# Cross-attention and routed experts on one core: projection columns reordered, query parts stacked from SBUF, the opening re-ordered

## The chip, the cores and the metric

The kernel runs on 1 core of one Trainium2 chip. The metric is the device time of one execution in microseconds (us), the median over runs. Engines: TensorE (PE), with its weight loads shown apart as PEld; VectorE (DVE); ScalarE (ACT); GpSimd (POOL); SyncE (SP), which here only issues transfers.

## What is computed

Sixteen batches of 112 rows and 256 columns attend to a context of 375 rows each; then every row goes through two of eight experts. Cut to what matters here:

```python
q = split_heads(layernorm(x) @ Wq.T + bq)      # 16 heads of 16 columns
k = split_heads(ctx @ Wk.T + bk)
v = split_heads(ctx @ Wv.T + bv)
scores = einsum('bhqd,bhkd->bhqk', q, k) / 4   # masked rows of ctx: -1e9
x = x + softmax(scores) @ v @ Wo.T + bo
x = x + top2_of_8_experts(layernorm(x))        # silu(x @ w1) @ w2, weighted
```

## The kernel before, in words

**Precision in parts.** Each operand of a product is cut into a high part and a low part (the rest), and a product is three matmuls: high x high, low x high, high x low. ACT writes high parts, DVE or POOL writes low parts.

**Stacked scores.** For a batch, the keys (`kh`, `kl`, 128 partitions x 2 x 376) are copied by DMA, SBUF to SBUF, into `ks[ring]`: 96 partitions hold (half of the heads, dimension of the head, part), and 8 head pairs lie along the row. The queries go into `qs[ring]` in the same way, so that one matmul of 98 rows gives a head's scores with all parts. Partitions 96 to 99 hold the mask and the row maxima. There are three rings. The keys take 6 transfers a batch (3 parts, each in 2 halves). The queries of the first batch take 6 transfers straight from SBUF; those of all others go through DRAM: `write_queries(g)` writes 6 pieces of a group of 4 batches to `q_scratch`, and `stack_queries` brings a batch back with 2 transfers. SP issues all of these in an order written by hand.

**Turns.** After the opening, PE runs a loop `turn(b)` over the 16 batches. In it lie the 16 `head_scores` of batch b+1 (DVE takes the maximum of each, `maxima`), the 4 `quad_scores` of batch b (ACT takes the exponentials), the outputs of b, the values of b+1 and the keys of b+3. The experts' stage follows after the last batch.

**The opening** (about the first 54 us) normalises x in 4 groups, transposes it, projects queries of the 4 groups, the keys of the first three batches and the values of the first, and takes the row maxima of the first batch. Each engine's order is a hand-written list of calls: `x_stats` (DVE), `x_std` (ACT, square root), `roots` (DVE), `normalise_x` (ACT), `x_transpose` (PE), `x_high` (ACT), `x_low` (DVE), `project_queries` (PE), `q_high` (ACT: `qf` and `qh`, both halves of the columns), `query_low` (POOL). `qf` is one buffer. `qh` and `ql` have two buffers each, so `q_high(g)` of groups 2 and 3 waits until the group before last has been written to DRAM. PE waits for all of `qh` before turn 0.

Of the kernel before, what the change touches and what calls it, by code (L numbers as in the profile page):

```python
# [5 lines left out]
F32 = mybir.dt.float32  # L6
# [21 lines left out]
GB = 4  # L28
# [77 lines left out]
def xattn_moe_kernel(nc, x_rows, x_tiles, ctx_t, mask, wq_t, wk_t, wv_t, wo_t, bq, bk, bv, bo,  # L106
                     router_w, w1, w2, out):
    ctx = ExitStack()
    with ctx:
# [19 lines left out]
        tl = sb("attn_t_lo", [P, KD, T], F32R)  # L129
        hidden_end = cursor["at"]  # L130
# [48 lines left out]
        def expert_buffers(p):  # L179
# [40 lines left out]
        qf = sb("q_f32", [P, KD, SG])  # L220
        qh = [sb(f"q_hi{p}", [P, KD, SG], F32R) for p in range(2)]
        ql = [sb("q_lo0", [P, KD, SG], F32R)]
        last_query_at = cursor["at"]
        ql.append(sb("q_lo1", [P, KD, SG], F32R))
# [6 lines left out]
        assert cursor["at"] <= xr_at + 4 * (B * D + KD * SG), "the last key stack lies where x and q were"  # L231
# [6 lines left out]
        assert cursor["at"] <= queries_end, "the third context lies where the queries' parts were"  # L238
# [88 lines left out]
        q_scratch = nc.dram_tensor("q_scratch", [KD, DK, PARTS, HALF, T], F32).ap()  # L327
# [9 lines left out]
        q_written = [sem(f"q_written{p}") for p in range(2)]  # L337
        bias_in, vo_bias_in, xr_first_in, xr_rest_in, rw_in = (sem(n) for n in (
            "bias_in", "vo_bias_in", "xr_first_in", "xr_rest_in", "rw_in"))
# [69 lines left out]
        def queries_stacked(b):  # L409

            return 48 * (b.lap + 1) + (64 if b.ring == 0 else 0)

        def queries_written(g):

            return 96 * (g // 2 + 1)

        def first_stack(queue, c, src):
            for a in range(2):
                row = PARTS * DK * a
                queue.dma_start(qs[0][row + c:row + PARTS * DK:PARTS, :, S * a:S * (a + 1)].bitcast(F32),  # L420
                                src[:, a, 0:S].bitcast(F32)).then_inc(q_stacked[0], 16)

        @block.sync
        def _(sp):
# [13 lines left out]

            def stack_queries(b):
# [5 lines left out]
                if not early(b, 1):  # L445
                    sp.wait_ge(q_written[b.n // GB % 2], queries_written(b.n // GB))
                    for a in range(2):
                        row = PARTS * DK * a
# [3 lines left out]
                if b.n == RINGS - 1:  # L452
                    sp.wait_ge(xt_done, NG)
                    sp.wait_ge(ql_ready, NG)
                sp.dma_start(ks[b.ring][R_MASK:ROWS, :, :].bitcast(F32),
                             mask_scratch[b.n:b.n + 1, :, :].rearrange("a p n -> p a n")
                             .to_broadcast([4, HALF, CP])).then_inc(q_stacked[b.ring], 16)

            def stack_keys(b):

                for c, src in enumerate((kh, kh, kl)):
                    if c != 1:
                        sp.wait_ge((kh_ready, kl_ready)[c // 2], b.n + 1)
                    for a in range(2):
                        row = PARTS * DK * a
                        sp.dma_start(ks[b.ring][row + c:row + PARTS * DK:PARTS, :, :].bitcast(F32),  # L466
                                     src[:, a, :].bitcast(F32)).then_inc(k_stacked[b.ring], 16)
# [9 lines left out]
            def turn(b):  # L477
                if has(b.after(2)):
                    stack_queries(b.after(2))
                    stack_keys(b.after(2))  # L480
                if b.n < 2:
                    write_queries(b.n + 2)
# [7 lines left out]
            def load_rows(group, done):  # L490
                sp.dma_start(xr[:, group, :], x_rows[group].rearrange("b s d -> s b d")).then_inc(done, 16)
# [4 lines left out]
            def write_queries(g):  # L496
                sp.wait_ge(qh_ready, KD * (g + 1))
                sp.wait_ge(ql_ready, g + 1)
                for c, src in enumerate((qh, ql, qh)):
                    for t in range(KD):  # L500
                        sp.dma_start(q_scratch[t, :, c, :, SG * g:SG * g + SG],  # L501
                                     src[g % 2][:, t, :].bitcast(F32)).then_inc(q_written[g % 2], 16)

            second = first.after(1)
            load_rows(slice(0, GB), xr_first_in)
# [5 lines left out]
            sp.dma_start(bv_c[:, :], bv).then_inc(bias_in, 16)  # L511
            sp.wait_ge(keep_ready, 1)
            sp.dma_start(keep_scratch, keep_all[:, :]).then_inc(mask_written, 16)
            load_rows(slice(GB, 2 * GB), xr_rest_in)
            sp.wait_ge(mask_written, 16)
            load_keep(0, slice(0, 2))
            load_ctx(second)
            load_weight(2, wv_t)
            sp.wait_ge(xr_rest_in, 16)
            load_rows(slice(2 * GB, B), xr_rest_in)  # L520
            sp.wait_ge(mask_rows_ready, 1)
            sp.dma_start(mask_scratch, m_rows[:, :, :].bitcast(F32)).then_inc(mask_written, 16)
# [1528 lines left out]
```

## Time and profile before

| | us |
|---|---|
| median of 3 runs | 471.98 (471.88 to 472.85) |
| profiled execution, its own time | 471.65 |
| its span in the profile | 469.9 |
| PE busy | 413.5 (88%) |
| DVE busy | 339.6 (72%) |
| ACT busy | 277.0 (59%) |
| POOL busy | 223.0 (47%) |

Times below are microseconds from the start of the span. A matmul's duration includes its overlap with the next one; the granted clock is given as a share of 2.4 GHz, so 0.50 is 1.2 GHz.

### The profile page before, as it was taken

How to read it: one execution, taken by the hardware profiler on the slowest of the kernel's cores; microseconds unless marked ns; L12 is line 12 of the kernel's file. 1: busy time of each engine (PE TensorE's matmuls, PEld its weight loads, DVE VectorE, ACT ScalarE, POOL GpSimd, SP SyncE). 2: the span in 40 equal slices, each digit the busy share in tenths (PEclk: the TensorE clock that was granted, in tenths of full speed). 3: DMA queues.
4: the chain of work that ended last, by engine and by line, in shares of the span. 5: the costliest groups of instructions: out<-in, count | busy, mean ns of one | idle time of the engine just before them, and what ended most of it. 6: DMA issues, size and time to landing. Idle time of an engine off the chain costs nothing.

```text
span 469.9 us, 10766 instructions
## 1 busy us (share of the span) xinstructions
PE 413.5 (88%) x4187; PEld 384.6 (82%) x4187; DVE 339.6 (72%) x699; ACT 277.0 (59%) x373; POOL 223.0 (47%) x252
## 2 busy tenths in 40 slices
PE   2767599999999999999999999589989999999820
PEld 2655489999999999999988898589989999999810
DVE  6746367878888787888877958965676777767545
ACT  3547356666655766565564462547767777788600
POOL 6554324332234444222322473844887787786420
PEclk9979889999999999999999996569999999999985
DMA  7999398867688777668670139912222222332169
GB/s 187 226 240 232 124 242 175 227 142 167 131 183 188 159 149 172 142 121 165 134 131 9 47 117 371 339 48 67 80 81 85 83 91 91 78 88 73 46 209 305
DMA packets 60307, 69.83 MB, mean 149 GB/s; under 512 B 19265, under 2 KB 55378, under 8 KB 60258
## 3 DMA queue, kind: packets, MB, share of 16 engines
q1 hardware_dynamic: 54018, 56.02, 49.1%
q0 software_dynamic: 4032, 11.02, 7.9%
q10 hardware_dynamic: 2208, 2.12, 1.3%
q8 instruction: 33, 0.54, 0.5%
q14 instruction: 16, 0.13, 0.1%
HBM read 35.29 MB, written 14.78 MB: 107 GB/s over the span
## 4 chain that ended last, share of the span: by engine, by line
PE 73%; DMA 8%; DVE 7%; issue 3%; ACT 3%; POOL 2%; SPq 2%; POOLq 0%; DVEq 0%; ACTq 0%
PE ps L1556 36%; PE ps L1617 11%; PE ps L1632 9%; PE ps L1646 9%; PE ps L1919 2%; PE ps L1659 1%; DMA q_scratch<-q_hi 1%; DMA k_stack<-k_lo 1%; DMA y_rows<-y_out,slot_of_row 1%; DMA w_raw<-wv_t 1%; DMA y_back<-y_rows 1%; SPq L501 1%; DMA rows<-xn_rows,token_of_row 1%; POOL rows L780 1%; SPq L466 1%
## 5 line engine op out<-in xcount | busy, mean ns | idle before, releaser
L1119 DVE TENSOR_REDUCE neg_max<-ps 112x1 f32<-112x376 f32 x256 | 133.5, 545 | 42.5 <-PE ps L1617 37.6
L852 ACT ACTIVATE probs<-ps 125x1344 f32<-125x1344 f32 x64 | 82.8, 1293 | 42.9 <-PE ps L1632 37.7
L1617 PE MATMUL ps<-k_stack,q_stack 98*112 98x376 f32 x256 | 87.5, 376 | 7.0 <-ACT q_hi L891 4.6
L619 POOL TENSOR_TENSOR k_lo<-k_f,k_hi 128x752 fp32r<-128x752 f32 x16 | 28.9, 1804 | 115.5 <-ACT k_hi L826 115.5
L780 POOL DMA_INDIRECT rows<-xn_rows,token_of_row x42 | 55.0, 1310 | 19.0 <-issue 12.2
L1617 PEld LDWEIGHTS ps<-k_stack,q_stack 98*112 98x112 f32 x256 | 45.3, 179 | 19.0 <-DVE neg_max L1119 9.9
L788 POOL DMA_INDIRECT y_rows<-y_out,slot_of_row x42 | 47.3, 1126 | 27.0 <-ACT y_out L1046 15.7
L1632 PE MATMUL ps<-q_stack,k_stack 100*125 100x224 f32 x384 | 53.0, 274 | 0.1
L1632 PEld LDWEIGHTS ps<-q_stack,k_stack 100*125 100x125 f32 x384 | 51.0, 190 | 0.9 <-ACT probs L852 0.5
L1556 PE MATMUL ps<-w_hi,h_hi 128*128 128x256 f32 x168 | 48.7, 290 | 1.6 <-issue 1.6
L1556 PE MATMUL ps<-flat_t_hi,w_hi 128*128 128x256 f32 x168 | 47.6, 283 | 2.0 <-DVE flat_t_lo L1443 2.0
L1556 PE MATMUL ps<-flat_t_hi,w_lo 128*128 128x256 f32 x168 | 47.2, 281 | 0.0
L1556 PE MATMUL ps<-flat_t_lo,w_hi 128*128 128x256 f32 x168 | 47.2, 281 | 0.0
L1556 PE MATMUL ps<-w_hi,h_lo 128*128 128x256 f32 x168 | 47.0, 280 | 0.0
L1556 PE MATMUL ps<-w_lo,h_hi 128*128 128x256 f32 x168 | 47.0, 280 | 0.0
L1646 PE MATMUL ps<-probs,v_wide 125*32 125x112 f32 x1536 | 47.0, 262 | 0.0
L1646 PEld LDWEIGHTS ps<-probs,v_wide 125*32 125x32 f32 x1536 | 35.1, 109 | 8.0 <-issue 5.6
L1027 ACT ACTIVATE h_f<-ps 128x1024 f32<-128x1024 f32 x21 | 21.6, 1027 | 25.8 <-PE ps L1556 25.8
L1556 PEld LDWEIGHTS ps<-flat_t_hi,w_hi 128*128 128x128 f32 x168 | 31.9, 190 | 2.4 <-DVE flat_t_lo L1443 2.4
L610 POOL TENSOR_TENSOR ctx_lo<-ctx_raw,ctx_hi 128x752 fp32r<-128x752 f32 x15 | 27.2, 1812 | 13.5 <-ACT ctx_hi L819 13.5
L1556 PEld LDWEIGHTS ps<-w_hi,h_hi 128*128 128x128 f32 x168 | 31.8, 189 | 2.0 <-issue 1.8
L1465 DVE TENSOR_TENSOR h_lo<-h_f,h_hi 128x1024 fp32r<-128x1024 f32 x21 | 25.7, 1225 | 10.2 <-ACT h_hi L1032 10.2
(209 smaller groups left out, 1023.6 us busy)
## 6 DMA issues: line engine op xcount, KB each, us to landing
k_stack<-k_hi SPq DMA_DIRECT2D x64, 188.0 KB, 4.6
w_all<-w SPq DMA_DIRECT2D x2, 4096.0 KB, 18.1
k_stack<-k_lo SPq DMA_DIRECT2D x32, 188.0 KB, 5.6
ctx_raw<-ctx_t SPq DMA_DIRECT2D x32, 187.5 KB, 5.1
q_stack<-q_scratch SPq DMA_DIRECT2D x30, 168.0 KB
q_scratch<-q_hi SPq DMA_DIRECT2D x16, 224.0 KB, 4.6
y_back<-y_rows SPq DMA_DIRECT2D x14, 256.0 KB, 4.8
q_scratch<-q_lo SPq DMA_DIRECT2D x8, 224.0 KB, 4.4
```

What stands on the lines that cost most here:

```text
L610: pool.tensor_tensor(cl[home][:, :, :], c_raw[b.par][:, :, :], ch[home][:, :, :].bitcast(F32), ALU.subtract).then_inc(cl_ready, 1)
L619: pool.tensor_tensor(kl[:, :, :], kf[:, :, :], kh[:, :, :].bitcast(F32), ALU.subtract)\
L780: pool.indirect_dma_start(rows[t.ring][:, a, :], None, xn_rows, row_of(token_i, t, a))\
L788: pool.indirect_dma_start(y_rows, row_of(slot_i, t, a), yo[t.par][:, a, :], None)\
L852: act.activation(pf[j % 2][:, :, :], ps[0:CT, BK_ST:BK_ST + KT, 0:4 * S], ACT.Exp).then_inc(pf_ready, 1)
L1027: act.activation(hf[t.par][:, :, :], silu_source(t), ACT.Silu).then_inc(hf_ready, 1)
L1119: dve.tensor_reduce(neg_max[:, s:s + 1], ps[0:S, BK_MAX + s % 2, 0:CP], AX.X, ALU.max, negate=True).then_inc(max_read, 1)
L1465: dve.tensor_tensor(hl[t.par][:, :, :], hf[t.par][:, :, :], hh[t.par][:, :, :].bitcast(F32), ALU.subtract).then_inc(hl_ready, 1)
L1556: last = pe.matmul(o, lhs, rhs, start=first and n == 0, stop=final and n == len(terms) - 1)
L1617: pe.matmul(ps[0:S, BK_MAX + a, 0:CP], qs[b.ring][0:R_MAX, q, S * a:S * (a + 1)], ks[b.ring][0:R_MAX, q, :], start=True, stop=True).then_i ...
L1632: last = pe.matmul(ps[0:CT, BK_ST + k3, 2 * S * q:2 * S * (q + 1)], ks[b.ring][0:ROWS, 2 * j + q, k3 * CT:(k3 + 1) * CT], qs[b.ring][0:ROW ...
L1646: last = pe.matmul(ps[VC * i:VC * (i + 1), BK_OUT, S * j:S * (j + 1)], vx[b.par][:, k3, 2 * j + i // 2 + HALF * (i % 2), :], pf[j % 2][:, ...
```

## The change

- The columns of the query and key weights and biases are put in another order (`by_dim`), so that a partition of the projected keys holds two head pairs that are neighbours in the stack. A key part is then one transfer over 128 partitions, 3 a batch and not 6.
- `q_scratch`, `write_queries` and the DRAM detour go. `qh` and `ql` now lie in the buffers `th` and `tl` (where the attention's output comes later), one place for each group, and a batch's queries are stacked from there by 6 transfers.
- The opening is re-ordered on all five engines. `q_high` and `first_query_low` are called by halves; keys of the first batch are cut before the value weights; the output weights and the router's weights are loaded, cut and their low parts taken before the first maxima; x comes in 4 loads; the table for exponentials is loaded behind the last square root; on PE the query products go ahead of the heads of the first batch; the wait for all of `qh` moves to the first `quad_scores`.
- PE runs 16 matmuls of the identity with itself, whose result is not read, ahead of the first transposes.

In the diff below, SP's part comes first, then ACT's list of the opening from the first keys on as it stands after the change, DVE's, PE's and the host's. The calls of `write_queries` for groups 1 to 3 go as the one shown does.

```diff
         def queries_stacked(b):
-            return 48 * (b.lap + 1) + (64 if b.ring == 0 else 0)
+            return 112 * (b.lap + 1)
...
+            def stack_part(b, c, src):
+                for a in range(2):
+                    row = PARTS * DK * a
+                    half = P // 2 * a
+                    sp.dma_start(qs[b.ring][row + c:row + PARTS * DK:PARTS, :, S * a:S * (a + 1)].bitcast(F32),
+                                 src[half:half + P // 2, :, S * b.n:S * (b.n + 1)].bitcast(F32))\
+                        .then_inc(q_stacked[b.ring], 16)
             def stack_queries(b):
...
-                        sp.dma_start(qs[b.ring][row:row + PARTS * DK, :, S * a:S * (a + 1)].bitcast(F32),
-                                     q_scratch[a, :, :, :, S * b.n:S * (b.n + 1)].rearrange("d c q n -> (d c) q n"))\
-                            .then_inc(q_stacked[b.ring], 16)
+                g = b.n // GB
+                sp.wait_ge(qh_ready, KD * (g + 1))
+                stack_part(b, 0, th)
+                stack_part(b, 2, th)
+                sp.wait_ge(ql_ready, g + 1)
+                stack_part(b, 1, tl)
...
             def stack_keys(b):
-                    for a in range(2):
-                        row = PARTS * DK * a
-                        sp.dma_start(ks[b.ring][row + c:row + PARTS * DK:PARTS, :, :].bitcast(F32),
-                                     src[:, a, :].bitcast(F32)).then_inc(k_stacked[b.ring], 16)
+                    sp.dma_start(ks[b.ring][c:KD * PARTS * DK:PARTS, :, :].bitcast(F32), src[:, :, :].bitcast(F32))\
+                        .then_inc(k_stacked[b.ring], 16)
...
-            write_queries(0)
...
             load_rows(2)
             sp.wait_ge(mask_rows_ready, 1)
             sp.dma_start(mask_scratch, m_rows[:, :, :].bitcast(F32)).then_inc(mask_written, 16)
+            load_weight(3, wo_t)
+            sp.dma_start(rw_raw[:, :, :], router_w.rearrange("k p n -> p k n")).then_inc(rw_in, 16)
+            sp.wait_ge(mask_written, 32)
+            stack_mask(first)
+            stack_keys(first)
+            stack_queries(first)
+            load_rows(3)
             load_ctx(first.after(2))
+            sp.wait_ge(filled, 4)
+            stack_queries(second)
+            stack_mask(second)
+            stack_keys(second)
...
+            key_high(first)
             attn_weight(2)
+            q_high(0, 0)
             x_std(1)
+            q_high(0, 1)
             normalise_x(1)
+            x_high(1)
             x_std(2)
+            normalise_x(2)
             key_high(second)
             attn_weight(3)
             act.wait_ge(rw_in, 16)
             act.copy(rw[:, :, 0:E], rw_raw[:, :, :]).then_inc(rw_ready, 1)
+            x_high(2)
+            values(first, True)
+            values(first, False)
+            x_std(3)
+            act.activation(root_c[:, :], eps_c[:, :], ACT.Exp)
+            q_high(1, 0)
+            normalise_x(3)
+            q_high(1, 1)
+            ctx_high(first.after(2))
+            q_high(2, 0)
+            x_high(3)
+            q_high(2, 1)
+            key_high(first.after(2))
+            q_high(3, 0)
+            q_high(3, 1)
...
+            attn_weight_low(2)
             x_stats(2)
+            roots(2)
             x_low(1)
+            attn_weight_low(3)
+            dve.wait_ge(rw_ready, 1)
+            dve.tensor_tensor(rw[:, :, E:2 * E], rw_raw[:, :, :], rw[:, :, 0:E].bitcast(F32), ALU.subtract)\
+                .then_inc(rw_ready, 1)
             maxima(first, range(0, 2))
...
+                    for n in range(16):
+                        pe.matmul(ps[:, BK_SPIN, 0:P], ident[:, :], ident[:, :], start=True, stop=True)
...
             for n, part in enumerate(all_parts):
+                project_queries(1, (part,))
                 head_scores(first, range(2 * n, 2 * n + 2))
-                project_queries(1, (part,))
             for n, part in enumerate(all_parts):
-                head_scores(first, range(8 + 2 * n, 8 + 2 * n + 2))
-                if n == 3:
-                    max_transpose(first)
                 project_queries(2, (part,))
                 if n == 2:
                     x_transpose(3)
+                head_scores(first, range(8 + 2 * n, 8 + 2 * n + 2))
+            max_transpose(first)
             for t in range(KD):
                 project_keys(first.after(2), t)
             project_queries(3)
-            pe.wait_ge(qh_ready, KD * NG)
...
     def by_dim(w):
-        return np.ascontiguousarray(w.reshape(w.shape[0], KD, HALF, DK).swapaxes(2, 3)).reshape(w.shape)
+        heads = w.reshape(w.shape[0], 2, HALF // KD, KD, DK)
+        return np.ascontiguousarray(heads.transpose(0, 3, 1, 4, 2)).reshape(w.shape)
```

## Rows read from the trace of the kernel before

**Rows 1.** The page: busy time, share and instructions; granted clock in 40 slices.

```profile
PE 413.5 (88%) x4187; PEld 384.6 (82%) x4187; DVE 339.6 (72%) x699; ACT 277.0 (59%) x373; POOL 223.0 (47%) x252
...
PEclk9979889999999999999999996569999999999985
```

**Rows 2.** Busy time by stretch: stretch, length, each engine, granted clock, DMA share, GB/s.

```profile
16.20:24.80 8.60, 6.14 (x40) 4.94 (x38) 7.41 (x25) 5.23 (x10) 6.42 (x6) 1.00 0.89 189
...
28.60:34.10 5.50, 5.46 (x19) 4.59 (x20) 3.10 (x6) 3.02 (x6) 4.42 (x3) 0.51 1.00 320
49.90:54.40 4.50, 0.00 (x0) 0.00 (x0) 0.00 (x0) 2.18 (x5) 0.00 (x0) 1.00 0.38 101
...
54.50:70.20 15.70, 14.16 (x97) 12.52 (x97) 11.34 (x20) 7.16 (x9) 6.78 (x10) 0.78 0.73 191
...
84.00:97.70 13.70, 13.70 (x177) 12.56 (x181) 11.01 (x25) 8.62 (x11) 3.56 (x2) 1.00 0.83 186
```

**Rows 3.** The chain of waits in order of time: start, duration, what.

```profile
21.45 5.64 DMA k_stack<-k_lo
...
46.49 5.66 DMA q_scratch<-q_hi
...
70.26 1.29 PE ps L1646 x48
...
83.99 1.29 PE ps L1646 x48
...
86.70 0.71 PE ps L1646 x24
```

**Rows 4.** Timeline: start, duration, engine, line, operation, tiles, idle time before.

```profile
12.98 0.52 PE L1556 MATMUL ps<-ctx_lo,attn_w_hi 128*128 128x376 f32 x1
...
13.76 0.34 PE L1556 MATMUL ps<-ctx_lo,attn_w_hi 128*128 128x376 f32 x1
...
15.26 1.49 DVE L1093 TENSOR_TENSOR attn_w_lo<-w_raw,attn_w_hi 128x512 fp32r<-128x512 f32 x1 [1.92 <-ACT attn_w_hi L803]
...
54.48 0.66 PE L1617 MATMUL ps<-k_stack,q_stack 98*112 98x376 f32 x1 [4.61 <-ACT q_hi L891]
54.50 2.10 POOL L643 TENSOR_TENSOR q_lo<-q_f,q_hi 128x896 fp32r<-128x896 f32 x1 [7.15 <-ACT q_hi L891]
...
54.97 2.18 DVE L1093 TENSOR_TENSOR attn_w_lo<-w_raw,attn_w_hi 128x512 fp32r<-128x512 f32 x1 [6.84 <-ACT attn_w_hi L803]
```

**Rows 5.** Timeline of SP's queue: start, time to issue, transfers.

```profile
10.34 0.55 SPq L522 DMA_DIRECT2D mask_scratch<-mask_rows  x1
...
18.15 2.61 SPq L466 DMA_DIRECT2D k_stack<-k_hi  x4
```

**Rows 6.** Transfers by line, first 62 us: count, KB each, median us to landing.

```profile
mask_scratch<-mask_rows SPq DMA_DIRECT2D x1, 94.0 KB, 8.1
```

**Rows 7.** ACT's groups of instructions, first 62 us: busy us, mean ns, idle before.

```profile
L875 ACT ACTIVATE x_rows_sb<-x_rows_sb,less_mean,rstd 112x256 f32<-112x256 f32 x12 | 6.2, 592 | 1.0 <-DVE less_mean L1167 1.0
L891 ACT ACTIVATE q_hi<-ps,bq_c 128x448 fp32r<-128x448 f32 x8 | 4.9, 628 | 0.0
...
L826 ACT CAST k_hi<-k_f 128x752 fp32r<-128x752 f32 x3 | 2.5, 819 | 7.3 <-DVE k_f L1103 4.3 <-DMA k_stack<-k_lo 3.1
...
L852 ACT ACT_TABLE_LOAD x1 | 1.3, 1283 | 0.0
```

**Rows 8.** The same view, DVE's groups.

```profile
L1119 DVE TENSOR_REDUCE neg_max<-ps 112x1 f32<-112x376 f32 x23 | 11.6, 541 | 8.7 <-PE ps L1617 8.4
L1156 DVE BATCH_NORM_STATS2 stats<-x_rows_sb 112x6 f32<-112x256 f32 x16 | 5.6, 409 | 1.7 <-DMA x_rows_sb<-x_rows 1.7
...
L1178 DVE TENSOR_TENSOR x_t_lo<-ps,x_t_hi 128x896 fp32r<-128x896 f32 x4 | 4.4, 1088 | 4.1 <-ACT x_t_hi L870 4.1
```

**Rows 9.** The same view, POOL's groups.

```profile
L643 POOL TENSOR_TENSOR q_lo<-q_f,q_hi 128x896 fp32r<-128x896 f32 x3 | 6.3, 2103 | 11.8 <-ACT q_hi L891 11.8
L619 POOL TENSOR_TENSOR k_lo<-k_f,k_hi 128x752 fp32r<-128x752 f32 x3 | 5.4, 1789 | 5.3 <-ACT k_hi L826 5.3
```

More of the change, by code:

```diff
@@ L129, in xattn_moe_kernel @@
         tl = sb("attn_t_lo", [P, KD, T], F32R)
+        qh = [th[:, :, SG * g:SG * (g + 1)] for g in range(NG)]
+        ql = [tl[:, :, SG * g:SG * (g + 1)] for g in range(NG)]
         hidden_end = cursor["at"]
@@ L219, in xattn_moe_kernel @@
         xr = sb("x_rows_sb", [S, B, D])
[L220 to L224, printed above, removed]
+        cursor["at"] = last_query_at = xr_at + 4 * (B * D + 4 * KD * SG)
+        cursor["at"] += 4 * KD * SG
         queries_end, cursor["at"] = cursor["at"], xr_at
@@ L230, in xattn_moe_kernel @@
         last_ring_end = cursor["at"]
-        assert cursor["at"] <= xr_at + 4 * (B * D + KD * SG), "the last key stack lies where x and q were"
+        assert cursor["at"] <= xr_at + 4 * (B * D + KD * SG), "the last key stack lies where x was"
         cursor["at"] = third_ctx_at = xr_at + first_queries
@@ L237, in xattn_moe_kernel @@
         third_ctx_end = cursor["at"]
-        assert cursor["at"] <= queries_end, "the third context lies where the queries' parts were"
+        qf = sb("q_f32", [P, KD, SG])
+        assert cursor["at"] <= queries_end, "the queries come before the flat rows"
         cursor["at"] = queries_end
@@ L488, in _, with load_rows @@
             first = Batch(0, 0)
-            def load_rows(group, done):
-                sp.dma_start(xr[:, group, :], x_rows[group].rearrange("b s d -> s b d")).then_inc(done, 16)
+            def load_rows(g):
+                group = slice(GB * g, GB * (g + 1))
+                sp.dma_start(xr[:, group, :], x_rows[group].rearrange("b s d -> s b d")).then_inc(xr_in[g], 16)
             def load_weight(n, w):
                 sp.dma_start(wraw[n], w.rearrange("k p n -> p k n")).then_inc(aw_in[n], 16)
[L496 to L502, printed above, removed]
             second = first.after(1)
-            load_rows(slice(0, GB), xr_first_in)
+            load_rows(0)
             sp.wait_ge(zeros_set, 1)
@@ L814, in ctx_high @@
                 else:
-                    if b.n == 6:
-                        for g in range(NG - 2, NG):
-                            act.wait_ge(q_written[g % 2], queries_written(g))
                     act.wait_ge(vproj_done, 2 * (b.n - 2))
@@ L1202, in _ @@
             keys(first, 0)
-            attn_weight_low(2)
             keys(first, 1)
@@ L1627, in quad_scores @@
                     pe.wait_ge(mx_stacked[b.ring], 32 * (b.lap + 1))
-                if not (early(b, 1) and j < 1):
+                if early(b, 1) and j < 1:
+                    pe.wait_ge(qh_ready, KD * NG)
+                else:
                     pe.wait_ge(pf_ready, QUADS * b.n + j)
```

126 lines of the change are left out of this document (34 added, 92 removed).

## The prediction

> **What bounds the kernel now.** I began with the page: PE is busy for 88% of the span, no other engine for more than 72% [rows 1]. The row of granted clock beneath it shows where PE is not at its best: three places, one near the start, one near the middle, one at the end [rows 1]. The change touches the first. In the stretches, a turn of the main loop takes 13.7 us, PE is busy for all of it and its clock is full [rows 2]. So in the turns nothing that another engine or a transfer does is worth time unless it comes too late. The opening is another matter: head 0 of turn 0 starts only at 54.48, after 4.61 us in which PE waited [rows 4]. In the stretch 49.90 to 54.40 PE does nothing at all [rows 2]. The chain of waits names what it waited for: a DMA into `q_scratch`, 5.66 us long, from 46.49 [rows 3], which kept `q_high(3)` from its buffer. Ahead of that the chain holds the last key part of the first batch, 5.64 us from 21.45 [rows 3]; ACT's `key_high(second)` stood behind it with the whole list that follows. After both, PE starts at half clock, 0.51 in 28.60 to 34.10 [rows 2]. Turn 0 shows what else is wrong: DVE's low part of the output weights is in the way of its maxima (2.18 us at 54.97 [rows 4]), and from head 0 to the outputs at 70.26 it takes 15.8 us at a mean clock of 0.78 [rows 2, 3, 4].
>
> The end of the change's reach is therefore that row at 70.26, where turn 1 begins in full swing. Every later turn is bound by PE, so what is gained there should reach the end unshortened.
>
> **The first 24 us.** The 16 unread products fill PE from the identity's making to about the first normalised rows. Before, matmuls of 376 columns took 0.52 us at 12.98 and 0.34 at 13.76 [rows 4]: that is where the clock rose. Some ten key products at half clock lie ahead of that, each about 0.15 us longer, so 1.5 us of PE time goes. It is hidden for the most part: the first keys also wait for the mask's broadcast, which lands no earlier. What moves the keys is the order: `k_f`'s second half now waits neither for the value weights nor for their low part (1.49 us from 15.26 [rows 4]), so I put `kh` of the first batch at 14.7 where its stacking began at 18.15 [rows 5]. It does not get all of this. SP now waits for `mask_scratch` first. That was issued at 10.34 and landed 8.1 us later, at 18.4 [rows 5, 6], behind 896 KB of x. Now 448 KB of it lie ahead, and at some 250 GB/s (the stretches show 189 to 320 [rows 2]) the other half is 1.8 us: 16.6. With the mask's own copy the keys begin at 17.2. Three transfers of 0.65 us each to issue [rows 5], not six. Their bytes are the same. Six took from 18.15 to 27.09, 8.9 us [rows 3, 5]; at the 189 GB/s of that stretch [rows 2] the 1.13 MB are 6.1. So they land between 23.3 and 26.1, and I take 24.2, near the lower end, since half of the issues and the DRAM writes behind them are gone. The second group's and third group's rows are normalised by about 24.0 on ACT, so nothing is lost by waiting.
>
> The Trainium skill bears on this (DMA: Bandwidth & Descriptors, Rules for kernel authors): two transfers to disjoint partition halves run one after the other over the same engines, so one transfer over 128 partitions is to be used. By that the keys' merger gives only issue time, and the queries' new halves cost issue time; no run here shows it yet, and neither the landing above nor the sum rests on it.
>
> **From 24.2 to turn 0.** One chain, each step by its row. ACT `kh` of the second batch 0.82, POOL `kl` 1.79 [rows 7, 9]; DVE's `attn_weight_low(3)` runs beside it. At 54.97 that operation took 2.18 us beside POOL's 2.10 from 54.50, so it ended 0.55 after POOL did [rows 4]: I let it end 0.55 after `kl`. With the router's parts 0.2: DVE is free for maxima at 27.6. The Trainium skill has the rule (SBUF — State Buffer, Who interferes with whom): a VectorE instruction with two SBUF inputs and a GpSimd one that reads SBUF block each other. The trace agrees, by the 2.18; without the rule this step would end about 1 us sooner. It speaks against putting the weights ahead of the maxima.
>
> DVE then: four maxima at 0.54, `x_low(2)` 1.09, `x_stats(3)` 1.4 and its aggregates 0.3 [rows 8], 5.0 in all: 32.6. ACT: square root 0.3, the exponentials' table 1.28 (it used to stand in turn 0 at no cost and is now on the path) and its dummy 0.2, `q_high(1,0)` 1.2, normalising four batches 2.07 (6.2 for 12), `q_high(1,1)` 1.2 [rows 7]: 6.3, so 38.9. PE has been held by `project_queries(2)`, which needs the banks that `q_high(1)` empties, and the heads 12 to 15 stand behind it. PE: one part 0.6, eight transposes 0.9, a pair of heads 0.35, four maxima 2.2, the transpose of the maxima 0.3: 43.2. Keys of the third batch, 12 products of 376 columns, 2.05, and queries of group 3, 12 of 448, 2.4, at full clock: 47.7. Beside it POOL does `query_low(1)` 2.1 and the third context's low part 1.8 [rows 9] from 38.9, ready at 42.8, just in time for the keys. The chain `q_high(2)`, `query_low(2)`, `q_high(3)` ends at about 48.9; the wait for it now stands at the first `quad_scores`, some 3.6 us into turn 0 (51.3), so it is covered by 2.4 us. The row maxima of the first batch are sent at 43.9 and needed there too. Head 0 of turn 0 starts at 47.7 for 54.48: **6.8 us**. The bounds of the key landing (23.3, 26.1) make it 7.7 or less to 4.9.
>
> **Turn 0.** A whole turn is 13.73 from 70.26 to 83.99 [rows 3]. Turn 0 has no outputs of a batch before, three times 0.71 [rows 3], nor its transposes, some 0.6. That is 11.0 of PE work. DVE has 16 maxima of 0.54 and two key halves, 9.9, and the first heads go at its pace. I take 12.2; the ends are 11.0 and 13.7. Before it was 15.8: **3.6 us** (2.1 to 4.8). The cover here is a warm PE, which has had no long pause since 42.
>
> **In the turns** PE has no slack but the rest has. SP issues 4 more query transfers (2.6 us by 0.65 each) and 3 fewer for keys (1.95): 0.65 us later, in a turn in which DMA is busy for 0.83 of 13.7 and so 2.3 us free [rows 2, 5]. Costed at nothing. The work that leaves (24 writes to DRAM) was on the path only at 46.49 [rows 3], counted above.
>
> Sum: 6.8 + 3.6 = 10.4. The profiled execution took 471.65, its span 469.9. 461.25; the median of the runs shown lies 0.33 above that execution: 461.6, which I round to 461.5.
>
> **Rivals.**
> *PE goes cold in the first batch's heads.* Between 25 and 37 it has short work between waits for DVE: some 5 us of 12. In 16.20 to 24.80 6.14 of 8.60 kept the clock at 1.00; 4.50 of nothing lost it [rows 2]; the case between is not in the trace. It would cost doubled parts, transposes and heads from 33 to 43, about 2.2, then the keys and queries of 43.2 on at half clock (the stretch at 0.51 lasted 5.5 us before the clock came back [rows 2], half of that lost: 2.7): 4.9, so 466.4. The Trainium skill (TensorE: Matmul & The Clock Gate, A second HAM failure mode) says that small idle times between groups of matmuls can make the clock go up and down; by that this rival is the forecast. I give it 0.2.
> *A wait takes the place of the one removed.* POOL's and ACT's query chain passes everything through one `qf`, and key landing at its upper end shifts it all by 1.9; if x of group 3, now loaded behind the first queries, comes after 31 as well, each us counts in full. 3 to 7 us of gain remain: 465 to 469. 0.13.
> *The gain is hidden.* That needs the third batch's keys to come late for turn 1: `kl` of it stands behind `query_low(3)`. I have it stacked at 58 for 59.9. For no gain at all it must be 12 us late. 0.03.
> *Slower: queries from SBUF overload the DMA in the turns.* 768 pieces a batch, now read from SBUF where 2 transfers read DRAM. It decides from 2.3 us more DMA work a turn on, and outweighs the opening above 3.1 (0.8 times 13 turns). At 3.5 it gives 461.5 + 13 x 1.2 = 477. For it: the DMA share of 0.83. Against it: the pieces are as many and as large as before, and the keys' pieces may become fewer. 0.06.
> *More than forecast:* turn 0 at 11.0 and keys at 23.3: 458. 0.08.
>
> **How the numbers follow.** Forecast 0.50, with its own range of 459 to 464. From the other cases: 457.5 below, 468 above leaves out some 0.15. Two runs of this kernel differ by up to 0.2%, 1 us, and less counts as no change. Faster by more than 0.2%: 0.89; within: 0.04; slower: 0.07.
>
> **What would show it.** Right: no row into `q_scratch`; PE busy from 2 us and key products at 0.34 from the first; head 0 of turn 0 near 47.7 at clock 1.00; the first maxima near 27.6; an idle PE around 36 to 38.9 waiting for `q_hi`; the x48 outputs near 59.9; turns of 13.7. Wrong: granted clock 0.5 between 27 and 45; a turn longer than 13.8 with PE waiting for a stack; first maxima after 29.

## The result, and the profile after

The kernel after takes 467.17 us (median of 4 runs, 466.05 to 468.23), the kernel before, measured beside it, 471.93 (4 runs, 471.34 to 472.85). The ratio is 0.9897, with a 95% interval of 0.9868 to 0.9926. So 4.8 us were gained where 10.4 were forecast. The profiled execution took 468.23, the longest of the four, with a span of 466.3 for the 469.9 of before. The readings below are made against that span.

The first lines to read are the same three of the page as in [rows 1]:

```profile
PE 418.5 (90%) x4219; PEld 388.8 (83%) x4219; DVE 340.3 (73%) x699; ACT 278.1 (60%) x374; POOL 223.4 (48%) x252
...
PEclk9868999999999999999999996569999999999965
```

They say little: PE is busy for 5 us more in a span 3.6 us shorter, and the first digits of the granted clock are lower, not higher. What tells more is the start of a turn in full swing, the x48 row of [rows 3]. In the chain of waits of the kernel after it comes at these times (start, duration, what):

```profile
61.68 1.29 PE ps L1622 x48
...
146.24 1.29 PE ps L1622 x48
...
231.58 1.29 PE ps L1622 x48
```

Turn 1 starts at 61.68 for the 70.26 of [rows 3]: 8.6 us gained in the opening. The row at 231.58 is twelve turns on: 169.9 us, 14.16 a turn on average, single ones 13.7 to 15.5. Before, a turn took 13.73 [rows 3], twelve of them 164.8. So 5.1 us of the 8.6 are lost again in the turns; 3.5 remain, and the spans differ by 3.6.

The chain shows the loss where a turn's first head is due, behind the x48 row:

```profile
161.32 1.70 issue
163.02 0.40 PE ps L1591
```

"issue" is time for which the view finds no releaser. The table of waits over 62 to 228 has it as the largest of PE's weight loads (us in total, times, longest):

```profile
PEld ps L1591 <- issue: 7.2, 12, 1.9
```

In the kernel before, and in the kernels below whose turns take 13.73, the same row reads 2.1 to 2.2 us. The excess over it is 5.1, the whole loss.

What PE waited for is read from SP's queue, here the transfers of the turn that starts at 146.24 (start, time to issue, transfers):

```profile
147.64 1.51 SPq L531 DMA_DIRECT2D x<-x_tiles  x1
149.24 2.57 SPq L437 DMA_DIRECT2D q_stack<-attn_t_hi  x4
151.86 1.25 SPq L437 DMA_DIRECT2D q_stack<-attn_t_lo  x2
153.15 0.49 SPq L429 DMA_DIRECT2D k_stack<-mask_scratch  x1
153.69 1.22 SPq L459 DMA_DIRECT2D k_stack<-k_hi  x2
154.96 0.61 SPq L459 DMA_DIRECT2D k_stack<-k_lo  x1
```

and from the landing time of the last of them (count, KB, us from issue to landing):

```profile
k_stack<-k_lo SPq DMA_DIRECT2D x1, 376.0 KB, 8.0
```

The keys' first transfer is issued at 153.69, 7.45 after the turn's start; the last, at 154.96, lands 8.0 later, at 162.96. The first head that reads them was due at 161.32 and ran at 163.02. In the kernel before, the same block stands like this in SP's queue, in the turn that starts at 152.62:

```profile
153.99 0.58 SPq L549 DMA_DIRECT2D x<-x_tiles  x1
154.67 1.92 SPq L449 DMA_DIRECT2D q_stack<-q_scratch  x2
156.63 0.51 SPq L455 DMA_DIRECT2D k_stack<-mask_scratch  x1
157.18 2.52 SPq L466 DMA_DIRECT2D k_stack<-k_hi  x4
159.75 1.25 SPq L466 DMA_DIRECT2D k_stack<-k_lo  x2
```

There the keys start 4.56 into the turn, and the last of its two `k_lo` transfers, 5.7 us on its way, lands at about 166.1, when the head is due at 167.6 (15.0 after the turn's start). Of the 2.9 us between 7.45 and 4.56, 1.9 are the queries' issues (3.82 for 1.92) and 0.9 the load of `x` ahead of them, which took 1.51 to issue here and 0.58 there. Over all twelve turns the keys start 5.9 to 7.7 us into the turn, 6.9 on average, where they started 3.2 to 4.8 in, 4.0 on average.

The reader should also see the cost of an issue: 0.64 us for 56 KB (2.57 for four), 0.61 for 376 KB. The transfer's size does not show in it, though a single issue can take more than twice as long, as that of `x` did. Meanwhile the DMA engines are not full. The stretch of the six query transfers and that of the keys behind it, one turn later (each engine's busy time, granted clock, DMA share, GB/s):

```profile
162.00:166.70 4.70, 3.68 (x45) 3.28 (x46) 2.33 (x5) 2.59 (x5) 2.79 (x2) 1.00 0.46 130
166.70:175.70 9.00, 9.00 (x95) 8.46 (x97) 7.92 (x18) 4.65 (x6) 2.02 (x2) 1.00 0.86 184
```

Over the twelve turns the DMA share fell, while the turns became longer. The kernel before and the kernel after:

```profile
70.26:235.09 164.83, 164.83 (x2081) 151.27 (x2084) 132.12 (x288) 102.82 (x130) 53.82 (x91) 1.00 0.75 161
61.68:231.58 169.90, 165.00 (x2080) 151.23 (x2084) 132.07 (x288) 103.71 (x130) 53.70 (x91) 1.00 0.66 148
```

SP's queue is not full either. The table of SP's own waits in the kernel after (us in total, times, longest) has one row over 62 to 228:

```profile
SPq L466 <- DVE max_rows L1103: 45.0, 12, 5.1
```

On average 3.75 us of each turn SP waits for the row maxima of the next batch, and the queries and keys of the batch behind it stand in the list after that wait. Whether they could be issued ahead of it was not tried.

The opening after the change, in pieces of the chain of waits:

```profile
9.96 5.86 DMA mask_scratch<-mask_rows
16.20 0.70 SPq L459
...
17.58 7.99 DMA k_stack<-k_lo
...
27.02 1.90 DVE attn_w_lo L1066
29.01 0.92 DVE neg_max L1092 x2
...
33.78 1.28 ACT L892
...
39.51 1.42 PE ps L1530 x3
...
44.30 4.56 PE ps L1530 x24
```

Each of these has its place in the forecast: the mask's landing, the keys, the low part of the output weights, the first maxima, the exponentials' table, a part of the query products of group 2, the keys of the third batch. Head 0 of turn 0 starts at 48.70 (54.48 in [rows 4]); 47.7 was forecast. The stretches show that PE did go cold on the way:

```profile
20.00:24.00 4.00, 4.00 (x24) 4.00 (x23) 2.60 (x11) 3.17 (x6) 1.94 (x2) 0.57 1.05 192
24.00:28.00 4.00, 1.91 (x10) 1.41 (x9) 0.98 (x1) 2.47 (x6) 1.41 (x1) 0.89 1.13 277
28.00:32.00 4.00, 3.85 (x11) 2.46 (x10) 4.00 (x8) 0.65 (x2) 3.49 (x3) 0.50 0.77 155
```

### The profile page after: what moved, and what is told of

The parts are those of the page before. It is cut to its first block, busy times and chain, and to the rows that moved or that the text cites. A ratio compares the mean times of both kernels' runs of the same rounds, so it can differ in the third digit from the quotient of the medians.

```text
span 466.3 us, 10813 instructions
## 1 busy us (share of the span) xinstructions
PE 418.5 (90%) x4219; PEld 388.8 (83%) x4219; DVE 340.3 (73%) x699; ACT 278.1 (60%) x374; POOL 223.4 (48%) x252
## 4 chain that ended last, share of the span: by engine, by line
PE 76%; DVE 8%; DMA 7%; issue 3%; ACT 3%; SPq 1%; POOL 1%; ACTq 0%; POOLq 0%; DVEq 0%
PE ps L1530 39%; PE ps L1591 12%; PE ps L1608 9%; PE ps L1622 9%; PE ps L1895 2%; DMA k_stack<-k_lo 2%; PE ps L1635 2%; DMA mask_scratch<-mask_rows 1%; DMA y_rows<-y_out,slot_of_row 1%; DMA y_back<-y_rows 1%; DVE neg_max L1092 1%; PE ps L1691 1%; DMA keep_scratch<-keep_all 1%; PE ps L1701 1%; PE ps L1647 1%
## 5 line engine op out<-in xcount | busy, mean ns | idle before, releaser
L1530 PEld LDWEIGHTS ps<-w_lo,h_hi 128*128 128x128 f32 x168 | 31.9, 190 | 0.0
```

What stands on the lines that cost most here:

```text
L1530: last = pe.matmul(o, lhs, rhs, start=first and n == 0, stop=final and n == len(terms) - 1)
```

## The experiments

All times are medians with their range; the ratio is to the kernel before on the same chip, with its 95% interval. The runs were spread over several chips, on which the median of the kernel before was 471.5 to 472.5, so kernels are compared by their ratios, and a difference of 1 us between two medians can be the chip's. "Head 0" is the start of head 0 of turn 0, "first row" the x48 row with which turn 1 begins in full swing.

### Where the turns lose: the order behind SP's queue

Three ways were open: the keys are issued too late (order), the merged key transfers land later than six small ones (size), or the DMA engines have too much to do (amount).

**Keys between the queries' parts.** From the first turn on SP issues the four high query transfers, then the keys, then the two low ones and the mask.

```diff
-                    stack_queries(b.after(2))
-                    stack_mask(b.after(2))
-                    stack_keys(b.after(2))
+                        stack_queries(b.after(2), low=False)
+                        stack_keys(b.after(2))
+                        stack_part(b.after(2), 1, tl)
+                        stack_mask(b.after(2))
```

> Edit: in the turns SP issues the four high query transfers, then the three key parts, then the two low query transfers and the mask; nothing else differs from the changed kernel. Theory A (the six query transfers stand ahead of the keys in SP's order and make the key stack land after head 0 of the next turn is due): the key parts are issued about 1.8 us earlier in a turn, head 0 no longer waits, all turns take 13.7 to 13.8 us, and the 5.1 us that twelve turns had lost come back: about 462 us. Theory B (one transfer of 376 KB for a key part is slow in itself, since its landing takes 7.1 us where 188 KB took 5.7): the block of keys still ends late and the turns stay uneven; under 1.5 us is gained, 466 to 467.

464.10 us (463.84 to 465.83, 4 runs); ratio 0.9845 (0.9809 to 0.9881). The first row comes at 61.22, the one twelve turns later at 227.94: 166.7, where the kernel after has 169.9. The same transfers in another order give back 3.2 of 5.1 us. The keys start 5.05 us into a turn on average for 6.9, and `k_lo` has a median of 6.1 us to landing for 7.1: the order acts through both. What is left has a name now:

```profile
PEld ps L1597 <- DMA k_stack<-mask_scratch: 3.2, 7, 0.9
```

The mask had been put last, and is late next. It was not tried alone; "Together" below moves it, and the rest of the loss is gone.

**Four query transfers fewer.** From the fourth batch on the high query parts are not stacked (left out of the computation); everything else stays in its order, so the keys come four issues earlier.

```diff
-                stack_part(b, 0, th)
-                stack_part(b, 2, th)
+                if early(b, RINGS):
+                    stack_part(b, 0, th)
+                    stack_part(b, 2, th)
```

> Leaves out part of the work: from the fourth batch on only the low part of the queries is stacked, the two high parts are not, so four of six query transfers of a turn are gone. Theory A: keys are issued 2.6 us earlier, every turn takes 13.7, about 462 us. Theory B: the keys are the same large transfers, so the turns stay uneven and it gives 465 or more.

463.49 us (462.73 to 463.86, 4 runs); ratio 0.9825 (0.9794 to 0.9855).

```profile
61.87 1.29 PE ps L1623 x48
...
226.60 1.29 PE ps L1623 x48
```

164.73 for twelve turns, 13.73 each: all of the loss is gone. Yet a `k_lo` transfer of 376 KB takes as long as in the kernel after: a median of 7.2 us for its 7.1.

So the size of the merged transfers is not what makes a turn long. As 224 KB a turn are gone as well as four issues, this kernel alone does not part order from amount.

**The column order and the merged key transfer alone**, in the kernel before; queries go through DRAM as there.

```diff
-                    for a in range(2):
-                        row = PARTS * DK * a
-                        sp.dma_start(ks[b.ring][row + c:row + PARTS * DK:PARTS, :, :].bitcast(F32),
-                                     src[:, a, :].bitcast(F32)).then_inc(k_stacked[b.ring], 16)
+                    sp.dma_start(ks[b.ring][c:KD * PARTS * DK:PARTS, :, :].bitcast(F32), src[:, :, :].bitcast(F32))\
+                        .then_inc(k_stacked[b.ring], 16)
```

> Edit to the kernel before: only the order of the projection's columns and the key part as one transfer; queries still go through DRAM, the opening is as it was. Theory A: the keys' block takes the same 8.9 us from its first issue to landing with three transfers as with six, nothing in the turns was waiting, so within 0.5 us of before: 471.5 to 472.4. Theory B: keys land later, some turns wait: 474 or more. My prediction's step for the opening (fewer issues make the first keys land earlier) would give 1 us less than before, 471.

470.44 us (468.93 to 471.71, 10 runs); ratio 0.9954 (0.9933 to 0.9976). In its profile head 0 comes at 52.55 and the first row at 68.30, 1.96 before that of [rows 3]; twelve turns take 165.26. In the opening the keys' first transfer is issued at 17.73 and the last lands at 25.69:

```profile
19.61 6.08 DMA k_stack<-k_lo
```

8.0 us for three transfers; six took 8.9 [rows 3, 5]. In the turns its `k_lo` has a median of 8.0 us to landing, the longest of all kernels here, and its turns are not slow: its keys start early. The merger lets the first block land 0.9 sooner, where three issues of 0.6 are saved, and gives about 0.5% of the time.

**Two transfers more.** The kernel after with two extra transfers of 56 KB to DRAM ahead of the keys in each turn.

```diff
                 stack_part(b, 1, tl)
+                if not early(b, RINGS):
+                    for a in range(2):
+                        sp.dma_start(extra[b.n, a], tl[P // 2 * a:P // 2 * (a + 1), :, S * b.n:S * (b.n + 1)].bitcast(F32))\
+                            .then_inc(q_stacked[b.ring], 16)
```

> Edit to the changed kernel: in the turns two more transfers of 56 KB (the low query parts, into a place in DRAM that nobody reads) stand ahead of the keys in SP's order, 1.3 us more to issue. Theory A (what stands ahead of the keys delays the end of the key stack, and head 0 of the next turn waits for it): every turn is now longer than 13.73, by 1 to 1.5 us, the alternating pattern becomes a steady one; twelve turns take 178 to 183 us, the time is 475 to 481. Theory B (the loss comes from the key transfers' own size or from other traffic): the twelve turns stay near 170 and the time near 467 to 469.

476.54 us (475.98 to 478.23, 4 runs); ratio 1.011 (1.007 to 1.0151). Twelve turns take 177.3 (63.21 to 240.47), 14.8 each.

```profile
PEld ps L1596 <- issue: 13.4, 14, 2.4
```

The same wait as in the kernel after, now 13.4 us for 7.2. Its `k_lo` still lands in 7.2 us, and the DMA share over the twelve turns is 0.66, as in the kernel after. Two transfers of 56 KB, 1.3 us of issue, cost 0.6 us a turn. With 2 query transfers ahead of the keys a turn takes 13.73, with 4 13.9, with 6 14.16, with 6 and the two extra ones 14.8 (the 13.9 is the mask's, as "Together" below shows: it has 4 ahead as well and turns of 13.73). The keys' first issue lies 4.0 to 4.1, 5.05, 6.9 and 8.2 us into the turn, on average.

### The opening: what is on the path

**No unread products.** The kernel after without the 16 products of the identity.

```diff
-                    for n in range(16):
-                        pe.matmul(ps[:, BK_SPIN, 0:P], ident[:, :], ident[:, :], start=True, stop=True)
```

> Edit: the changed kernel without the 16 unread products. I expect the first key products at half clock again (0.31 us apart and not 0.17), and the first keys as late as the mask's broadcast lets them be (13.4), so the time within 1 us of the changed kernel, 466.5 to 468. If the clock was on the path, it is 1.5 to 2 us slower than the changed kernel: 468.5 to 469.5.

468.11 us (466.81 to 471.30, 10 runs); ratio 0.9936 (0.9912 to 0.9960). Its interval overlaps that of the kernel after (0.9868 to 0.9926); the span is the same, 466.3, and head 0 comes at 48.57 for 48.70. The products are worth nothing that can be measured here. Its turns are those of the kernel after, and twelve of them took 168.8 in its profile (61.53 to 230.33) for 169.9: the loss differs by 1 us from one execution to the next.

**Output weights ahead of the second batch's keys on ACT**, in the kernel with the keys between.

```diff
-            key_high(second)
             attn_weight(3)
             act.wait_ge(rw_in, 16)
             act.copy(rw[:, :, 0:E], rw_raw[:, :, :]).then_inc(rw_ready, 1)
+            key_high(second)
```

> Base: e1_keys_between. ACT cuts the output weights and the router's before it waits for the key stack (key_high of the second batch), not behind it. Then DVE's low part of the output weights (1.90 us at 27.02, beside POOL's k_lo) runs at about 24.8 while DVE idles, in 0.7 us. If that step was on the path as my prediction has it, the first maxima start 1.1 us earlier (at 27.8 and not 28.9, then bound by the last query transfer that landed at 27.3) and head 0 of turn 0 comes 1 us earlier: 463. If the clock or the ACT chain behind takes it back, 464.

463.80 us (462.45 to 465.62, 4 runs); ratio 0.9837 (0.9794 to 0.9881), in which it can't be told from the kernel it is built on. In the trace it did its work: the first maxima come at 28.07 for 28.81, head 0 at 47.75 for 48.24.

**The exponentials' table back in turn 0.**

```diff
-            act.activation(root_c[:, :], eps_c[:, :], ACT.Exp)
```

> Base: e1_keys_between. The dummy exponential that loads the table behind the last square root is left out, so the table is loaded at the first real exponentials, as before the change. My prediction put its 1.48 us on the path: then head 0 of turn 0 and the time come up to 1.5 us earlier, 462.6, since ACT waits for PE at the first exponentials anyway. If the load now delays the first exponentials, as the author of a preload would hold, nothing or a loss up to 1.3 us: 464 to 465.4.

462.45 us (462.27 to 462.65, 4 runs); ratio 0.9804 (0.9772 to 0.9837). Head 0 comes at 47.73, 0.5 earlier. The median falls by 1.65, but the intervals of the two ratios overlap (0.9809 to 0.9881 for the kernel it is built on). Only a third of the 1.5 us between the two spans shows in the opening; the rest lies in turns that wait less for the mask (2.4 us in that row for 3.2) and behind the turns. In the trace ACT did come earlier: `q_high(1,1)` ends at 38.00 for 39.19. But PE, at half clock, reaches the query part that waits for it only at 38.77, for 39.70, and stays at half clock almost to the end of that part.

**Together:** keys between, output weights first, table late, and in each turn the mask ahead of the queries and the load of `x` (for the experts) behind the context's.

```diff
+                if mask:
+                    stack_mask(b)
                 sp.wait_ge(qh_ready, KD * (g + 1))
```

> Base: e1_keys_between with both edits of e6 and e7, and in the turns the mask's transfer ahead of the queries and the load of x for the residual behind the context's, since head 0 still waits up to 0.9 us in some turns for the mask, which is now the last in the order. Expected: twelve turns in 164.8 us (e1: about 166.7), 2 us less, and 1 to 2.5 us from the opening: 460 to 461. If the opening's two edits have the same place on the path, 461.5.

459.83 us (459.29 to 460.17, 4 runs); ratio 0.9750 (0.9717 to 0.9783). Twelve turns take 164.8 again (58.52 to 223.29), with all six query transfers and all bytes, at a DMA share of 0.63: the whole loss of the turns is one of order. Its keys start 4.9 us into a turn on average.

Head 0 comes at 45.43, 2.8 us before that of the kernel with the keys between, where the two edits of the opening gave 0.5 each alone. 1.0 of it is there at the first maxima (27.78 for 28.81). From these to head 0 it takes 17.65 us, for 19.43 in the kernel with the keys between, 19.68 with the output weights first and 18.60 with the table late. The granted clock is the difference that the rows show, here in 36 to 40 of the kernel with the table late and of this one:

```profile
36.00:40.00 4.00, 4.00 (x15) 3.57 (x14) 2.01 (x4) 2.71 (x5) 1.86 (x1) 0.54 1.03 312
36.00:40.00 4.00, 3.51 (x19) 2.56 (x19) 2.24 (x5) 2.42 (x5) 3.18 (x2) 1.00 0.98 298
```

In the first PE is busy for all 4 us and stands in the chain of waits; in the second it waits for ACT.

**The mask's rows ahead of two loads.** The write of `mask_scratch` goes ahead of the value weights and of the third group of x (704 KB).

```diff
+            sp.wait_ge(mask_rows_ready, 1)
+            sp.dma_start(mask_scratch, m_rows[:, :, :].bitcast(F32)).then_inc(mask_written, 16)
             load_weight(2, wv_t)
             load_rows(2)
-            sp.wait_ge(mask_rows_ready, 1)
-            sp.dma_start(mask_scratch, m_rows[:, :, :].bitcast(F32)).then_inc(mask_written, 16)
```

> Base: e8_together. In the opening SP writes the mask to DRAM ahead of the value weights and of the third group of x, not behind them. In e8 the write went out at 10.28 and landed at 16.0, and the keys' first transfer stood behind it (16.38). If the landing of the first stacks is what the opening waits for (my prediction's step), the first key transfer goes at about 15.3 (kh is ready then), everything to turn 0 moves by 0.8 to 1 us: 459. If DVE's or ACT's list is the bound, no change: 459.8. The value weights come 0.5 us later, which could take some of it back.

457.17 us (456.40 to 457.71, 4 runs); ratio 0.9680 (0.9647 to 0.9713): the fastest kernel of the study, 15 us below before and 10 below after; its interval lies clear of that of "Together" (0.9717 to 0.9783). SP's queue in its opening:

```profile
12.54 0.32 SPq L429 DMA_DIRECT2D k_stack<-mask_scratch  x1
...
17.25 0.55 SPq L462 DMA_DIRECT2D k_stack<-k_lo  x1
```

SP no longer waits for the mask but for the keys themselves, and `k_lo` lands in 5.7 us (7.7 in the kernel it is built on). The first maxima come at 25.41 for 27.78, head 0 at 43.70 for 45.43. The chain of waits has no key transfer left between 10 and 30, and the output weights' low part is short:

```profile
24.67 0.69 DVE attn_w_lo L1072
...
25.45 0.97 DVE neg_max L1098 x2
```

**PE kept busy.** In the kernel "together", unread products of 64 columns between the heads of the first batch: 16 ahead of the first pair, 3 ahead of or behind later ones, into a free bank (the profile counts two matmuls for each). The last ones, behind the heads, are not in the diff shown.

```diff
             for n, part in enumerate(all_parts):
                 project_queries(1, (part,))
+                if n == 1:
+                    pe.wait_ge(vx_ready, 2)
+                unread(3 if n else 16, 6 if n else BK_SPIN)
                 head_scores(first, range(2 * n, 2 * n + 2))
```

> Base: e8_together. 16 unread products of 64 columns while PE waits for the first stacked queries (25.2 to 27.1), and 3 after each of the next pairs' query products, so that PE is not idle between the first batch's heads. My rival said that the cold clock there costs 4.9 us. In e8 the clock is 0.50 in 28 to 32 and 0.84 in 32 to 36, and PE has some 15 products of 448 columns at 0.37 apart and not 0.20 there: 2.5 us of PE time, most of it beside DVE's maxima. If DVE and ACT set the pace, the clock comes to 1.00 and the time stays within 0.5 us of e8 (459.3 to 460.3); if the clock is on the path, 457.5 to 458.5.

460.97 us (460.44 to 461.04, 4 runs); ratio 0.9764 (0.9733 to 0.9794), in which it can't be told from the kernel it is built on (0.9750); nothing is gained. The clock is full:

```profile
28.00:32.00 4.00, 4.00 (x31) 3.88 (x29) 2.96 (x6) 0.27 (x1) 3.74 (x3) 1.00 0.61 159
32.00:36.00 4.00, 3.45 (x19) 2.72 (x18) 3.60 (x14) 2.42 (x6) 0.00 (x0) 1.00 1.05 200
```

but the products themselves are in the way of the first heads:

```profile
25.12 3.68 PE L1820 MATMUL ps<-ident 128*128 128x64 f32 x32
28.60 0.57 PE L1597 MATMUL ps<-k_stack,q_stack 98*112 98x376 f32 x2
```

The first maxima come at 29.04 for 27.78. From the first maxima to head 0 it takes 17.91 us at full clock and 17.65 in the kernel "together", whose clock there was 0.50 and 0.84 in the same two stretches. In "Together" the chain of waits from the first maxima to 36.82 holds DVE and ACT rows alone, so the half clock up to there cost it nothing. For a kernel in which PE stays at half clock beyond that, this run is no test: its own unread products stand in the chain, twice 0.62 us between 36.27 and 38.51, and can have taken what the clock gave:

```profile
37.89 0.62 PE ps L1820 x6
38.51 0.67 PE ps L1536 x3
```

The query part at 38.51 takes 0.67 us at full clock, where the kernel after has 1.42 at 39.51.

**The table at the end of ACT's opening**, behind `q_high(3, 1)`.

```diff
             q_high(3, 1)
+            act.activation(root_c[:, :], eps_c[:, :], ACT.Exp)
```

> Base: e8_together. The dummy exponential comes at the end of ACT's opening, where ACT idles 1.6 us (46.9 to 48.5 in e8), instead of at the first real exponentials (48.85, with the exponentials at 50.14 and PE waiting 0.66 for them). Expected 0.6 to 1 us less in turn 0: 459.0. If turn 0 goes at DVE's pace, 459.8.

459.33 us (458.73 to 459.68, 4 runs); ratio 0.9724 (0.9693 to 0.9755).

```profile
47.26 1.28 ACT L909 ACT_TABLE_LOAD   x1
...
49.86 1.29 ACT L833 ACTIVATE probs<-ps 125x1344 f32<-125x1344 f32 x1 [0.64 <-PE ps L1615]
```

The exponentials start at 49.86 for 50.14 and wait for PE, not for the table, but head 0 and the first row come no earlier (45.83 and 58.63). The intervals overlap: no gain that can be told.

**All of these together**, unread products included.

> Base: e8_together with the edits of e9, e10 and e11. If all three are on the path, 457.0 to 458; if only the table is, 459.

460.76 us (459.90 to 461.19, 4 runs); ratio 0.9762 (0.9731 to 0.9793). Head 0 comes at 47.01, the first row at 59.82, as with the unread products alone (46.95 and 60.01): they take back all that the mask's early rows give.

## Why the prediction was right or wrong

**The step that failed is "In the turns": "0.65 us later, in a turn in which DMA is busy for 0.83 of 13.7 and so 2.3 us free. Costed at nothing."** It cost 5.1 us in the profiled execution. The DMA share was read as slack. It says nothing on when a transfer is issued, and the 0.65 was the difference of all issues of a turn, while what counts is what stands ahead of the keys: six queries' transfers for two, 2.6 us of issue, and the keys start 6.9 us into a turn on average and not 4.0 (7.45 and 4.56 in the two turns shown). The block of keys needs 8.9 us from its first issue before (157.18 to 166.1) and 9.3 after (153.69 to 162.96), and its first head is due 15.0 after the turn's start. Before, 15.0 - 4.6 - 8.9 left 1.5 us in that turn. After, 7.45 + 9.27 - 15.02 is 1.70 too late, which is the wait in the chain. In the kernel after the share even fell (0.66 over twelve turns for 0.75), and the turns became longer. The orders tried settle it: same transfers in another order, 3.2 of 5.1 back; in yet another ("Together"), all back; fewer ahead, all back; more ahead, 7.4 more lost over twelve turns. A turn that is held up gives the keys issued in it that much more time, so it is mostly every second turn that is long. The longest, 15.47, is a turn of 13.76 and this wait of 1.70, behind the load of `x` that took 1.51 to issue; why that one took so long was not settled. The prediction had named the sign, "a turn longer than 13.8 with PE waiting for a stack", and it is what came.

**The slower rival** ("queries from SBUF overload the DMA in the turns") named the right place and the wrong quantity. It asked for 2.3 us of DMA work; what decided was a margin in the order, of 1.5 us in the turn shown and 2.1 by the average start of 4.0. It would have been found by timing the keys against their head, with the rows of SP's queue.

**The opening, 10.4 forecast, 8.6 measured.** The direction and most of the size were right, by the mechanism forecast: no row into `q_scratch`, and PE's wait ahead of head 0 gone. Head 0: 5.8 for 6.8. The step that failed here is the keys' landing. The mask came early, at 15.8 for 16.6, and the keys were issued from 16.2 for 17.2, but the block took 9.4 us (16.20 to 25.57) where I took 7.0 "near the lower end, since half of the issues and the DRAM writes behind them are gone". Even the upper bound of 8.9 was too short. The reason given for the lower end was half right: the merger alone lands the block in 8.0 for 8.9, so fewer issues do help, by 0.9. But in the opening as re-ordered the same three transfers took 9.4, and what held them there was not settled. From there the forecast runs 1.3 behind at the first maxima (28.94 for 27.6), makes up 0.5 on DVE and 0.5 on ACT, and loses 0.5 on PE, where parts and heads at a lower clock took 4.8 us for 4.35 (39.3 to 44.13). The third batch's keys and the queries of group 3 took 4.57 for 4.45, at full clock as forecast. Turn 0: 13.0 for 12.2, because PE waited 0.86 for the low part of a context:

```profile
57.27 0.41 PE L1530 MATMUL ps<-ctx_hi,attn_w_hi 128*128 128x376 f32 x1 [0.86 <-issue]
```

POOL had it done only at 57.17, behind a key part of 1.80 that it had started at 53.62:

```profile
55.38 1.79 POOL L592 TENSOR_TENSOR ctx_lo<-ctx_raw,ctx_hi 128x752 fp32r<-128x752 f32 x1
```

**The output weights ahead of the maxima** went as forecast. `attn_weight_low(3)` took 1.90 from 27.02 and ended at 28.92, 0.55 after POOL's `k_lo` (26.59 to 28.37). The rule of the Trainium skill (SBUF — State Buffer, Who interferes with whom), by which a VectorE instruction with two SBUF inputs contends with a GpSimd one that reads SBUF, agrees with the runs: with no POOL instruction beside it the same operation took 0.69.

**The table on the path** was right in kind: without it ACT is 1.2 us earlier, but head 0 only 0.5, for the 1.48 that the step counted, since PE at half clock became the bound behind it. The fall of the median by 1.65 is not that step's: two thirds of it lie in the turns and behind them.

**"PE goes cold in the first batch's heads"** did occur (0.50 in 28 to 32), and cost little of the 4.9 it was priced at: the clock was back at 1.00 for the keys of the third batch, for which 2.7 was counted, and of the 2.2 counted ahead of them some 0.5 shows in the step from 39.3 to 44.13. Most of the stretch goes at the pace of DVE and ACT. The Trainium skill says that small idle times between groups of matmuls can make the clock go up and down (TensorE: Matmul & The Clock Gate, A second HAM failure mode): the rows of 20 to 32 fit that, with 0.57, 0.89 and 0.50 in a row, but the time followed only in part.

**The merged transfers.** The Trainium skill (DMA: Bandwidth & Descriptors, Rules for kernel authors) has two rules that bear on the change. That two transfers to disjoint partition halves run one after the other, so that one is to be used, fits the merger: 8.0 us for 8.9, ratio 0.9954, no more than the issues saved. The other one, that many small transfers are to be coalesced since under 64 KB one pays mostly overhead, speaks against the queries' six transfers of 56 KB. I did not weigh it. The runs show its advice to be right through the issue of 0.64 us each; an overhead in the DMA engines they do not show, whose share fell.

## What to carry to other kernels

What the DMA engines' busy share leaves free is no slack: time each transfer of a repeated block from its first issue to its landing against the instruction that needs it, and put what is needed first first in the issuing queue. Here a transfer cost its issuer the same 0.6 us whether it brought 56 or 376 KB, so splitting something that is not urgent can still delay what is urgent behind it. And before paying to keep TensorE's clock up, see in the chain of waits whether the stretch goes at TensorE's pace at all; an edit that speeds up another engine can make it so, and then gives less than its own time.

## What the runs showed of the hardware

- The issue on SP of a stacking transfer takes mostly 0.60 to 0.66 us, for 56 KB as for 376 KB; single issues took longer, as the load of `x` with 1.51 for 0.58.
- Three transfers of 376 KB land little sooner than six of 188 KB: 8.0 (merger alone) and 8.9 us for the same 1.13 MB in the opening, and in the turns about 9 us from the first issue in either form. Medians of a single `k_lo` went from 6.1 to 8.0 us over these kernels, by what stood around it, and the turn's length did not follow them.
- Moving a 94 KB transfer ahead of 704 KB of loads gave 2.7 us of median (ratio 0.9680 for 0.9750), though the keys behind it were issued only 0.5 to 1.0 earlier: `k_lo` then landed in 5.7 us for 7.7. Why it did was not settled.
- Half the clock while the chain of waits went through DVE and ACT cost nothing that shows ("Together": 0.50 in 28 to 32, and 17.65 us from the first maxima to head 0). With the table late, where PE was still at half clock when its own products came into the chain (0.54 in 36 to 40), the same way took 18.60 us. No run parts the clock's share in this cleanly.
